# Mixing product of the condition gate in three fp32r products instead of one fp32 product

## The reference

```python
cond = einsum('bct,bcd->bdt', x, L0_cond_weights[itok_B_0_15])   # 32x32 matrix per sequence
q_c  = cond @ Wq_c.T + bq_c                                      # 192 features
kv   = cond @ Wkv_c.T + bkv_c                                    # 64 latent + 64 rope features
# 32 heads: q from q_c, k and v from kv, softmax over the 32 tokens, output projection
x = x + attention
x = x + ffn(long_convolution(x))                                 # taps from sin/exp of a state space model
```

## Time and profile before

| | us |
|---|---|
| median of 3 runs | 736.43 |
| lowest and highest | 736.04, 737.22 |
| the profiled execution, its whole time | 739.18 |
| its span in the trace | 737.3 |
| PE busy in it | 707.4 (96%) |
| DVE busy | 589.8 (80%) |
| ACT busy | 412.7 (56%) |
| POOL busy | 205.9 (28%) |

### The profile page before, as it was taken

How to read it: one execution, slowest core, us unless ns; L and a number is a source line. 1 busy time by engine, 2 the same in 40 slices (tenths; PEclk the granted TensorE clock), 3 DMA queues, 4 the chain that set the end, 5 groups by cost and what they waited for, 6 DMA issues and landing times.

```text
span 737.3 us, 17037 instructions
## 1 busy us (share of the span) xinstructions
PE 707.4 (96%) x7152; PEld 568.3 (77%) x7152; DVE 589.8 (80%) x1010; ACT 412.7 (56%) x736; POOL 205.9 (28%) x237
## 2 busy tenths in 40 slices
PE   8999999999999999999999999999989799999997
PEld 7767787786978788787869787887667687777785
DVE  5778989998997877697767868777987688788754
ACT  5576565655656765846555565648554444444433
POOL 5361020030002010540300000006200176766676
PEclk9999999999999999999999999999999999999999
DMA  7800100010002001000100010012112678888732
GB/s 224 316 3 2 58 5 1 2 62 2 2 1 63 2 2 58 2 4 13 61 2 2 1 59 2 1 32 74 44 63 49 180 196 207 196 210 182 181 99 101
DMA packets 31919, 50.94 MB, mean 69 GB/s; under 512 B 6594, under 2 KB 21090, under 8 KB 30562
## 3 DMA queue, kind: packets, MB, share of 16 engines
q1 hardware_dynamic: 29858, 49.26, 24.4%
q0 software_dynamic: 1024, 0.53, 0.3%
q10 hardware_dynamic: 960, 0.06, 0.1%
HBM read 41.19 MB, written 8.63 MB: 68 GB/s over the span
## 4 chain that ended last, share of the span: by engine, by line
PE 85%; DVE 8%; ACT 2%; issue 2%; DMA 1%; POOL 1%; SPq 0%; POOLq 0%
PE ps L719 34%; PE ps L611 7%; PE ps L768 7%; PE ps L612 7%; PE ps L613 6%; PE ps L790 5%; PE ps L660 3%; PE ps L1012 3%; PE ps L1017 3%; PE ps L619 2%; PE ps L621 2%; PE ps L620 2%; DVE sum_low L1666 2%; PE ps L988 1%; DVE z_low L1393 1%
## 5 line engine op out<-in xcount | busy, mean ns | idle before, releaser
L1112 ACT ACTIVATE qt<-ps,m_bias 128x512 f32<-128x512 f32 x228 | 145.9, 686 | 88.9 <-PE ps L719 79.6
L719 PE MATMUL ps<-q_high,m_high 64*128 64x512 f32 x768 | 166.6, 398 | 0.6 <-issue 0.3
L719 PE MATMUL ps<-q_high,m_low 64*128 64x512 f32 x768 | 162.3, 388 | 0.0
L719 PE MATMUL ps<-q_low,m_high 64*128 64x512 f32 x768 | 114.2, 387 | 0.0
L719 PEld LDWEIGHTS ps<-q_high,m_high 64*128 64x128 f32 x768 | 89.7, 185 | 16.2 <-issue 6.5
L719 PEld LDWEIGHTS ps<-q_high,m_low 64*128 64x128 f32 x768 | 89.7, 185 | 9.6 <-issue 0.6
L1393 DVE TENSOR_TENSOR z_low<-ps,z_high 128x512 fp32r<-128x512 f32 x128 | 79.7, 681 | 17.8 <-ACT z_high L1132 16.4
L719 PEld LDWEIGHTS ps<-q_low,m_high 64*128 64x128 f32 x768 | 81.5, 184 | 10.0
L1132 ACT CAST z_high<-ps 128x512 fp32r<-128x512 f32 x128 | 66.7, 597 | 13.7 <-PE ps L790 9.2
L1117 ACT ACTIVATE sc<-sc 128x512 f32<-128x512 f32 x60 | 38.1, 635 | 41.5 <-DVE sc L1378 35.9
L600 POOL TENSOR_TENSOR y_low<-y,y_high 128x512 fp32r<-128x512 f32 x32 | 46.8, 1461 | 41.3 <-ACT y_high L1322 41.3
(11 more groups left out here) (251 smaller groups left out, 1470.5 us busy)
## 6 DMA issues: line engine op xcount, KB each, us to landing
x_raw<-in_x_groups SPq DMA_DIRECT2D x32, 256.0 KB
x_t<-in_x_channels SPq DMA_DIRECT2D x8, 1024.0 KB, 8.2
out<-rest SPq DMA_DIRECT2D x32, 256.0 KB, 5.1
toep_high<-taps_scratch SPq DMA_DIRECT2D x32, 192.0 KB, 4.2
toep_low<-taps_scratch SPq DMA_DIRECT2D x32, 192.0 KB, 4.7
w_raw<-in_w_groups SPq DMA_DIRECT2D x8, 512.0 KB, 7.2
toep_far<-taps_scratch SPq DMA_DIRECT2D x32, 64.0 KB, 5.1
rope_raw<-in_rope_rows SPq DMA_DIRECT2D x8, 192.0 KB, 7.3
```

The source lines that it names most:

```text
L719: mm = pe.matmul(ps[:, fold_bank(u, j) + e, :], weights[rows, (GH * g + j) // 2, c, :], moving[c][rows, :], start=start, stop=stop)
L1112: act.activation(qt[:, j, :], ps[:, fold_bank(u, j) + j % 2, :], ACT.Identity, bias=m_bias[:, h:h + 1]).then_inc(s["qt_done"], 1)
```

## The change

Group 0 keeps the old product (`mix_first`). From group 1 on:

- ACT's `feat_taken` writes fp32r `feat_high` and raises `feat_rounded` in place of `feat_done`.
- DVE gets a new `feat_rest(k, n)` after each `below_max(u, n)`: PSUM minus `feat_high` into `feat_low`, in pieces of 320 and 64 columns; it raises `feat_done`.
- DVE's `angles(*turn)` in the odd half steps moves from ahead of `projected_ab` to behind `crossed`.
- POOL gets `mask_cut(k)` after `masked(k)`: two copies that round `mix` to `mix_high` and two subtractions that make `mix_low`.
- PE's `mix_features(k)` does 36 fp32r products instead of 12 fp32 ones. The product that raises `q_ready` is the 23rd, the one for `qca_ready` the 24th, the one for `kv_ready` the 36th.
- The chain of five `kind_step` waits and one `row_step` at DVE's start uses the shared counter `step` instead; ACT waits for `step` 6.

```diff
-            def mix_features(k):
-                pe.wait_ge(s["feat_done"], 4 * k + 4)
-                pe.wait_ge(s["mix_ready"], 2 * k + 2)
...
+            def mix_features(k):
+                pe.wait_ge(s["feat_done"], 4 * k + 3)
+                pe.wait_ge(s["mix_cut"], 4 * k)
+                pe.wait_ge(s["s_taken"], 4 * (2 * k - 1) + 3)
+                pe.wait_ge(s["zl_done"], 8 * (2 * k - 1))
+
+                def by_high(part, n):
+                    out_n, left = mixed_in(part)[:, P * n:P * n + P], feat_high[:, n, P * part:P * part + P]
+                    pe.matmul(out_n, left, mix_high[n // 2][:, n % 2, :], start=True, stop=False)
+                    pe.matmul(out_n, left, mix_low[n // 2][:, n % 2, :], start=False, stop=False)
+
+                def by_low(part, n):
+                    return pe.matmul(mixed_in(part)[:, P * n:P * n + P], feat_low[:, n, P * part:P * part + P],
+                                     mix_high[n // 2][:, n % 2, :], start=False, stop=True)
+
+                for part in range(2):
+                    for n in range(3):
+                        by_high(part, n)
+                        by_low(part, n)
+                    if part == 0:
+                        pe.wait_ge(s["feat_rounded"], 4 * k)
+                    by_high(part, 3)
+                pe.wait_ge(s["feat_done"], 4 * k + 4)
+                by_low(0, 3).then_inc(s["q_ready"], 1)
+                by_low(1, 3).then_inc(s["qca_ready"], 1)
+                for n in range(4):
+                    by_high(2, n)
+                    mm = by_low(2, n)
+                mm.then_inc(s["kv_ready"], 1)
...
+            def mask_cut(k):
+                if k == 1:
+                    pool.wait_ge(s["fold_ready"], QUADS)
+                pool.wait_ge(s["kv_ready"], k)
+                pool.wait_ge(s["mix_ready"], 2 * k + 2)
+                for j in range(2):
+                    pool.tensor_copy(mix_high[j][:], mix[j][:]).then_inc(s["mix_cut"], 1)
+                for j in range(2):
+                    pool.wait_ge(s["mix_cut"], 4 * (k - 1) + j + 1)
+                    pool.tensor_tensor(mix_low[j][:], mix[j][:], f(mix_high[j][:]), ALU.subtract).then_inc(s["mix_cut"], 1)
...
+            def feat_rest(k, n):
+                dve.wait_ge(s["feat_rounded"], 4 * (k - 1) + n + 1)
+                dve.tensor_tensor(feat_low[:, n, 64:64 + FEAT], ps[:, FEAT_BANK[n], 0:FEAT], f(feat_high[:, n, 64:64 + FEAT]),
+                                  ALU.subtract)
+                dve.tensor_tensor(feat_low[:, n, 0:64], ps[:, FEAT_BANK[n], P:QL], f(feat_high[:, n, 0:64]),
+                                  ALU.subtract).then_inc(s["feat_done"], 1)
...
                     for n in range(4):
                         below_max(u, n)
-                    angles(*turn)
+                        feat_rest(i // 2, n)
                     projected_ab(i // 2)
                     projected_ca(i // 2)
                     crossed(i // 2)
+                    angles(*turn)
```

More of the change, by code:

```diff
@@ L175, in build @@
                       for n in (0, 2, 1)] for k, part in enumerate(("high", "low")))
+    mix_high = [t(f"mix_high{n}", [P, 2, P], F32R, at=c_at + (5 + n) * KB) for n in range(2)]
+    mix_low = [t(f"mix_low{n}", [P, 2, P], F32R, at=at) for n, at in enumerate((c_at + 7 * KB, c_at))]
+    feat_high = t("feat_high", [P, 4, 64 + FEAT], F32R, at=qt_at + 24 * KB)
+    feat_low = t("feat_low", [P, 4, 64 + FEAT], F32R, at=qt_at + 8 * KB)
     wcT_high = t("wcT_high", [P, TT, FEAT], F32R, at=wcT_at)
@@ L271, in build @@
                     "wcT_done rope_high fold_ready fold_high fold_done wvT_high_done wvT_done "
-                    "block_rows row_step row_ready blocks_ready mix_ready bias_done mb_done").split()
-    attention_names = ("xh_done xl_done feat_ready feat_done q_ready kv_ready "
+                    "block_rows row_ready blocks_ready mix_ready mix_cut bias_done mb_done").split()
+    attention_names = ("xh_done xl_done feat_ready feat_rounded feat_done q_ready kv_ready "
                        "qca_ready q_high_done q_crossed q_done q_copied kv_done ct_ready ct_done t_ready qt_done s_ready s_taken "
@@ L514, in front @@
                     masked(u // 2 + 1)
+                    if u >= 2:
+                        mask_cut(u // 2 + 1)
                     if u + 4 < NU:
@@ L550, in _ @@
                 values_low(n)
+            mask_cut(1)
             for u in range(1, 7):
@@ L1051, in feat_taken @@
                 act.wait_ge(s["feat_ready"], 4 * k + n + 1)
-                act.copy(feat[:, n, 64:64 + FEAT], ps[:, FEAT_BANK[n], 0:FEAT])
-                act.copy(feat[:, n, 0:64], ps[:, FEAT_BANK[n], P:QL]).then_inc(s["feat_done"], 1)
+                if k == 0:
+                    act.copy(feat[:, n, 64:64 + FEAT], ps[:, FEAT_BANK[n], 0:FEAT])
+                    act.copy(feat[:, n, 0:64], ps[:, FEAT_BANK[n], P:QL]).then_inc(s["feat_done"], 1)
+                else:
+                    act.copy(feat_high[:, n, 64:64 + FEAT], ps[:, FEAT_BANK[n], 0:FEAT])
+                    act.copy(feat_high[:, n, 0:64], ps[:, FEAT_BANK[n], P:QL]).then_inc(s["feat_rounded"], 1)
             def projected_ab(k):
@@ L1443, in _ @@
             dve.wait_ge(s["block_rows"], 4)
[L1444 to L1454, removed]
+            chain(dve.tensor_tensor(row_in_block[:], l_pos, block_row[:], ALU.subtract))
+            chain(dve.tensor_copy(row_kind[:], l_pos))
+            chain(dve.tensor_scalar(row_kind[:], row_kind[:], 3, None, ALU.bitwise_and))
+            chain(dve.tensor_scalar(unit_of[:], row_kind[:], 1.0, None, ALU.is_equal))
+            chain(dve.tensor_scalar(bits_of[:], unit_of[:], 4032.0 - 63.0, 63.0, ALU.mult, ALU.add))
+            chain(dve.tensor_scalar(unit_of[:], unit_of[:], 1.0 / 64.0 - 1.0, 1.0, ALU.mult, ALU.add))
             dve.wait_ge(s["cond_in"], 16)
```

13 lines of the change are left out of this document (7 added, 6 removed).

## The result

The change made the kernel slower: 758.71 us (median of 4 runs, 757.89 to 760.27) against 736.83 (4 runs, 736.04 to 737.88). The ratio is 1.0300, 95% interval 1.0281 to 1.0319, so +21.9 us. The forecast was 751 us with a range of 740 to 757: the direction was right, the size was 7.7 us too small, and the result lies 1.7 above the range.

What follows compares the result with a forecast made beforehand. The prediction took PE to bound the kernel, with DVE next. Products 9.4 us plus waits 5.3 us made 14.7 us over the median of 736.43, forecast 751 us, range 740 to 757.

Steps and rivals of the forecast that it cites:

- The products: PE's mixing: 36 fp32r products at 0.112 us replace 24 records of 2.68 us; 1.35 us a group, 9.4 over 7 groups.
- Rival 1: Mixing on PE: the weight load doesn't bind, products flow at 0.064 us, waits grow to 6.6; 740.4 us, chance 0.06.
- Rival 3: Mixing on PE: weight loads overlap in part, 0.088 us a product, waits of 3.4 and 2.5; 745.7 us, chance 0.04.
- Rival 4: Mixing on PE: a narrow fp32r product is carried out as two records, 0.223 us; 776 us, chance 0.06.
- rival 2: Faster than before: mixing products at 0.064 us and PE doesn't meet the DVE chain; 733.8 us, chance 0.04.
- The waits as such: PE waits for DVE ahead of the second `values` part: 3.1 us in group 1, 2.2 in group 2.
- Rival 5: Only the PE products term, no waits for DVE: 745.8 us, chance 0.09.
- q's later start: `q_ready` comes with the 23rd mixing product instead of the 8th record, 1.68 us later; no new wait in PE's fold.
- `mask_cut` on POOL is four operations in a wait of some 30 us: nothing: POOL's new mixing cuts fit into its existing wait and cost nothing, also for the gather behind it.
- After its wait PE carries on from the moment that DVE is ready: Behind the `values` waits PE and DVE are shifted alike, so neither wait is won back; the waits total 5.3 us.
- So they cost PE nothing: `feat_rest` on DVE, at most 3.9 us a group, ends before PE's 23rd mixing product needs it; no cost.
- The wait term: Angle steps moved behind `crossed` delay DVE, so PE waits 3.1 and 2.2 us in groups 1 and 2; 5.3 us.

Runs made afterwards that it cites:

- e2_angles_behind_alone: The kernel before with only the angle steps moved, from ahead of `projected_ab` to behind `crossed`: 745.77 us, ratio 1.0130.
- e5_cut_later: The kernel after with POOL's `mask_cut` held until DVE has taken the first scores of the next half step: 755.02 us, ratio 1.0246.
- e3_two_products: The kernel after with the angle steps back ahead of `projected_ab` and the high x low products left out (24 products, not 36): 745.44 us, ratio 1.0109.
- e6_half_moving: The kernel after with the angle steps back ahead of `projected_ab` and mixing products on 64 of 128 moving columns: 751.3 us, single run.

## Why the prediction was right in part, and where it failed

**The products: right.** The price of 0.112 came from two rows that showed the load's share in other places, and it was 0.1117. The term was 9.4 and measured 9.6. Rivals 1 and 3 (0.064, 0.088) and 4 (0.223) are excluded by the distance of the starts, rival 2 by them and by the time.

**The waits as such: right.** 3.1 and 2.2 were forecast from sums of adjacent DVE rows, and with `mask_cut` away from the angle steps they are 3.16 and 2.15. That it fits to 0.06 is in part luck: the same sums were half a microsecond short in e2_angles_behind_alone. Rival 5, no waits, is excluded by the two waits in the trace of after and by that run.

**q's later start: right.** q_low was to start 3.59 after the mixing (1.91 + 1.68) and did so 3.44 after it in group 2.

**"`mask_cut` on POOL is four operations in a wait of some 30 us: nothing": this step failed.** The cover was real for POOL's own time: nobody waits for POOL. But the operations start on `kv_ready`, exactly when DVE works through the moved angle steps, and POOL's operations slow DVE's. I looked for who waits for the engine and not at what runs beside it. It cost 2.5 us. The same step hid group 3, for which I allowed "perhaps some tenths" (0.51).

**"After its wait PE carries on from the moment that DVE is ready": this step failed too.** It treats PE's speed as given. The granted clock had been 1.00 throughout the stretch that I read the earlier trace rows, and PE never stood idle in it; the change makes it stand idle, and the clock fell behind both waits, 3.0 us. The trace of before had no idle of that size in the group steps, but it had two in its last stage, and the clock fell at the end of each. A row of PE's timeline and a window of before show the first; the second is 3.85 us of idle up to 580.20 and half clock from 580.4:

```profile
543.13 1.16 PE L790 MATMUL ps<-pT,ctok 32*64 32x128 f32 x32 [2.85 <-DVE sc_last L1572]
```

```profile
542.95:546.30 3.35, 3.17 (x70) 2.68 (x72) 1.33 (x2) 1.95 (x4) 0.00 (x0) 0.50 0.03 5
```

So the cost could be bounded from the record of before; I didn't look there, and the range had no bound for it.

**"So they cost PE nothing", of the features' low parts: right here, but by a cover that the change itself makes.** With the 36-product mixing and the angle steps behind, they are hidden. With 24 products and the angle steps ahead they cost 3.3 to 5.0 us.

**The numbers.** The wait term was mis-sized, 5.3 for a measured 10.8 (5.3 + 2.5 + 3.0). 751.1 plus those 5.5 is 756.6; 0.2 more for the products, the 0.2 that the table leaves, the 0.4 by which the median of before was higher beside the result (736.83 for 736.43) and the 1.3 that only the medians show make it 758.7. The upper end of 757 was made of a dearer product (2.6), new waits on PE (2.1), neither of which occurred, and 1.2 to spare; a bound for slowed DVE rows and for the clock would have taken in the result.

## What to carry to other kernels

With narrow products, count weight loads, not columns: 128 weight columns held the next product for 0.112 us with 128 moving columns and with 64, so three products in place of two records add half of the mixing's time. Before you put a wait on an engine that had none, price it as idle time and again as slower matmuls behind it, 1.3 to 1.7 us here for each fall of the clock. And before you call an operation on POOL free, look at which DVE rows run beside it: twice their usual time is possible.

## What I had not expected of the hardware

- POOL's elementwise operations and DVE's slow each other. DVE: 0.69 to 1.11, 0.43 to 0.85, and a 64-partition copy 0.42 to 0.85. POOL: two subtractions 1.43 to 2.33.
- The length of a wait didn't decide about the clock: 3.35 us of idle left it at 1.00 (e2_angles_behind_alone, group 1), 2.39 (the same run, group 2) and 2.15 (e5_cut_later, group 2) were followed by a fall. Shorter waits were too: 0.47, 0.16 and 0.77 within 2 us in the fold of e3_two_products, while a single 1.23 (the same run, group 2) was not. What decides is left open.
- The clock also fell without idle time, in the mixing with 64 moving columns of e6_half_moving. The row of a stretch around it (PE busy throughout, mean granted clock 0.75) and the starts at the point of the fall:

```profile
361.00:369.00 8.00, 8.00 (x48) 6.83 (x46) 4.90 (x9) 2.50 (x4) 2.52 (x5) 0.75 0.40 131
```

```profile
364.78 0.28 PE L692 MATMUL ps<-mix_high,feat_low 128*128 128x64 f32 x1
...
365.22 0.40 PE L692 MATMUL ps<-mix_high,feat_low 128*128 128x64 f32 x1
365.44 0.40 PE L688 MATMUL ps<-mix_high,feat_high 128*128 128x64 f32 x1
```

The starts go from 0.11 to 0.22 apart, so the pace that the weight load sets halves with the clock as well. It is one run, in which two groups fell; the full-width mixing of the other runs never did.
